# Four of the seven middle-sized tables looked up by TensorE in place of two, with the known rows in two buffers

## The reference, cut to what matters

```
e = stack([tbl_f[ids[:, f]] for f in range(50)], axis=1)      # 2048 x 50 x 16
z = einsum('bid,bjd->bij', e, e)[:, I, J]                     # pairs i < j: 1225
h = concatenate([z, dense_ctx], axis=1)                       # 1241
h = maximum(h @ W_top1 + b_top1, 0)                           # 512
h = maximum(h @ W_top2 + b_top2, 0)                           # 256
y = h @ W_top3                                                # 1
```

## Time and profile before

| | |
|---|---|
| three runs | 480.82, 483.11, 483.5 us |
| the profiled execution | 480.74 us, its span 478.8 us |
| mean granted TensorE clock | 0.857 of 2.4 GHz |
| PE / weight load busy | 332.1 / 233.1 us |
| DVE busy | 279.6 us |
| ACT busy | 196.2 us |
| POOL busy | 329.2 us |
| chain that ended last, by engine | PE 22%, SP queue 22%, DVE 14%, ACT 14%, DMA 9%, POOL 8%, issue 8% |

### The profile page before, as it was taken

The page is one execution under the profiler, slowest core; times in us unless marked ns, Lnnn a source line. Parts: engine busy times, 40 slices in busy tenths (PEclk is TensorE's granted clock), DMA queues, the critical chain, the costliest instruction groups (busy, mean ns, idle before and its releaser), DMA issues.

```text
span 478.8 us, 12641 instructions
## 1 busy us (share of the span) xinstructions
PE 332.1 (69%) x5432; PEld 233.1 (49%) x5432; DVE 279.6 (58%) x538; ACT 196.2 (41%) x269; POOL 329.2 (69%) x320
## 2 busy tenths in 40 slices
PE   0576154672978698889886697887969475574772
PEld 0576154662665466657654566565634142333331
DVE  3688599993543888484736967655342725435220
ACT  1427412543246544354483347344671322404020
POOL 5777878777777777777777777777777777750000
PEclk9768575886979979799997799999889797977798
DMA  6995332332222334222223322111212112120100
GB/s 190 404 344 156 109 95 60 75 100 62 65 69 51 101 92 105 79 81 56 54 73 103 86 52 48 40 35 38 60 15 62 37 40 52 21 62 3 58 1 0
DMA packets 24872, 38.70 MB, mean 81 GB/s; under 512 B 8784, under 2 KB 16240, under 8 KB 24688
## 3 DMA queue, kind: packets, MB, share of 16 engines
q1 hardware_dynamic: 14340, 34.80, 21.9%
q0 software_dynamic: 9984, 2.58, 6.1%
q10 hardware_dynamic: 492, 0.51, 0.3%
HBM read 26.79 MB, written 0.13 MB: 56 GB/s over the span
## 4 chain that ended last, share of the span: by engine, by line
PE 22%; SPq 22%; DVE 14%; ACT 14%; DMA 9%; POOL 8%; issue 8%; POOLq 0%; another core or an unknown queue 0%; ACTq 0%; DVEq 0%
SPq L358 22%; PE hid_ps L711 9%; POOL emb L426 8%; DVE onehot L460 6%; ACT gram L790 6%; PE look_ps L685 5%; DMA ids_bc<-ids_dram 5%; PE mid_ps L739 4%; ACT z_both L839 3%; PE gram_ps L702 3%; DMA z_both<-dense 2%; DVE turned L565 2%; ACT looked L809 2%; DVE z_both L522 1%; DVE w_sb L637 1%
## 5 line engine op out<-in xcount | busy, mean ns | idle before, releaser
L426 POOL DMA_INDIRECT emb<-tbl,gidx x312 | 328.4, 1053 | 97.4 <-issue 93.0
L711 PE MATMUL hid_ps<-w_sb,z_both 127*128 127x512 f16 x528 | 131.0, 398 | 17.0 <-DVE z_both L522 17.0
L685 PE MATMUL look_ps<-parts,onehot 125*128 125x64 f16 x1836 | 79.3, 207 | 67.0 <-DVE onehot L460 51.8
L685 PEld LDWEIGHTS look_ps<-parts,onehot 125*128 125x128 f16 x1836 | 73.2, 108 | 80.1 <-issue 37.0
L790 ACT ACTIVATE gram<-gram_ps 50x784 f32<-50x784 f32 x112 | 91.4, 816 | 45.1 <-PE gram_ps L702 41.7
L460 DVE TENSOR_SCALAR onehot<-ids_bc,rows 125x2048 f16<-125x2048 f16 (+1 forms) x144 | 92.4, 692 | 18.5 <-PE look_ps L685 14.7
L711 PEld LDWEIGHTS hid_ps<-w_sb,z_both 127*128 127x128 f16 x528 | 49.6, 102 | 76.3 <-DVE z_both L522 17.9
L702 PE MATMUL gram_ps<-turned 32*128 32x100 f16 x2048 | 37.4, 213 | 39.7 <-ACT gram L790 28.1
L809 ACT ACTIVATE looked<-look_ps 128x1024 f16<-128x1024 f32 (+1 forms) x28 | 26.7, 955 | 87.4 <-PE look_ps L685 87.3
L702 PEld LDWEIGHTS gram_ps<-turned 32*128 32x128 f16 x2048 | 27.0, 97 | 49.4 <-ACT gram L790 31.4
L460 DVE TENSOR_SCALAR onehot<-ids_bc,rows_med 125x1024 f16<-125x1024 f16 x75 | 34.6, 496 | 27.6 <-PE look_ps L685 27.5
(11 more groups left out here) (43 smaller groups left out, 128.9 us busy)
## 6 DMA issues: line engine op xcount, KB each, us to landing
ids_bc<-ids_dram SPq DMA_DIRECT2D x28, 512.0 KB, 4.1
emb<-tbl,gidx POOLq DMA_INDIRECT x312
z_both<-gram SPq DMA_DIRECT2D x31, 121.0 KB
z_both<-w SPq DMA_DIRECT2D x1, 2816.0 KB
z_both<-gram SPq DMA_DIRECT2D x31, 90.8 KB
z_both<-gram SPq DMA_DIRECT2D x155, 6.2 KB
z_both<-gram SPq DMA_DIRECT2D x31, 60.5 KB
gram<-small SPq DMA_DIRECT2D x2, 512.0 KB, 4.9
```

The costliest lines, as they stand in the source:

```text
L426: pool.indirect_dma_start(emb[:, T % TPC, f, :], None, big[f], bass.IndirectOffsetOnAxis(ap=gidx[:, T, f:f + 1], axis=0)).then_inc(gathere ...
L685: last = nc.tensor.matmul(bank[:, half, at:at + width], onehot[0:TP, at_ring, i, t * TILE:(t + 1) * TILE], moving.rearrange("p i s d -> p ...
L711: return nc.tensor.matmul(hid_ps[:, :], z_parts[0:KP, T % 2, x, k, :], w1_sb[0:KP, k, w, :], start=(i == 0), stop=(i == L1_MM - 1))
```

## The change

`NM` goes from 2 to 4: tables 26 and 27, the third and fourth in `MED`, are looked up by PE from chunk 1 on. Tiles 4 to 15 gather 17 fields in place of 19. A chunk from 1 on has 86 slices in place of 61 and 10 groups in place of 9, a slot 21 or 22 slices. `RING` goes to 5, `EARLY` to 14 and `MIDDLE` to 18.

The memory for this comes from other buffers. `looked` and `looked_med` become one ring of three groups (`LOOKS`), and a move of a group to its home follows two groups after its copy, in the chunk before the one that uses it. `split` becomes `known`, two halves by chunk parity, for rows that are looked up (and one gathered field that shares their last pair), and `fresh`, one tile's gathered rows for each of four tiles. The third copy is gone: the second transpose reads the two parts in reverse order. `odd` has two halves, loaded one chunk further ahead. The staging of the medium tables takes four places, two of them inside `parts_med`.

```diff
-NM = 2
+NM = 4
-RING = 6
+RING = 5
+LOOKS = 3
+JL = JS + JM + 1
-EARLY = 11
-MIDDLE = 13
+EARLY = 14
+MIDDLE = 18
-MOVES = ((0, 1), (2, 3), (4, 5), (6, 7), (8,), (), (), ())
-        odd = sb("odd", [128, TPC, PICK_BITS], I32)
+        odd = sb("odd", [128, 2, TPC, PICK_BITS], I32)
-        looked = sb("looked", [128, NG, 2, TPC, 2, PR, WORDS], F16)
-        looked_med = sb("looked_med", [128, NGM, MGRP, TPC, PRM, WORDS], F16)
+        looked = sb("looked", [128, LOOKS, 2 * TPC * 2 * PR * WORDS], F16)
-        split = sb("split", [128, TPC, JJ, 3, DIM, 2], F16)
+        known = sb("known", [128, 2, TPC, JL, 2, DIM, 2], F16)
+        fresh = sb("fresh", [128, TPC, JJ - JL, 2, DIM, 2], F16)
-        med_f32 = (parts_med[:, 1, :].bitcast(F32), gram[:, 0, 0:KM * DIM])
+        med_f32 = (parts_med[:, 1, :].bitcast(F32), gram[:, 0, 0:KM * DIM],
+                   parts_med[:, 3, :].bitcast(F32), gram[:, 1, 0:KM * DIM])
+        MED_HOME = (0, 2, 1, 3)
...
             def load_sample_ids(n):
-                if n > 0:
-                    sp.wait_ge(picked, FIRST_GROUP[n])
+                if n >= 2:
+                    sp.wait_ge(picked, FIRST_GROUP[n - 1])
...
+            load_sample_ids(1)
             for o in range(IDS_BUFS, FIRST_GROUP[1]):
                 load_ids_bc(o)
...
-            sp.dma_start(med_f32[0], med[:, 0, :]).then_inc(med_in[0], 16)
+            for m in (0, 2):
+                sp.dma_start(med_f32[m], med[:, MED_HOME[m], :]).then_inc(med_in[m], 16)
...
-            sp.dma_start(med_f32[1], med[:, 1, :]).then_inc(med_in[1], 16)
+            for m in (1, 3):
+                sp.dma_start(med_f32[m], med[:, MED_HOME[m], :]).then_inc(med_in[m], 16)
             for T in range(NTILES):
-                if T % TPC == 0 and T // TPC + 1 < NCH:
-                    load_sample_ids(T // TPC + 1)
+                if T % TPC == 1 and T // TPC + 2 < NCH:
+                    load_sample_ids(T // TPC + 2)
...
+            def homes(T):
+                t, half = T % TPC, T // TPC % 2
+                runs = [(emb[:, t, NM, :], known[:, half, t, JL - 1, :, :, 1])]
+                runs += [(emb[:, t, NM + 1 + a:NB:2, :], fresh[:, t, :, :, :, a]) for a in range(2)]
+                if T < TPC:
+                    runs += [(emb[:, t, a:NM:2, :], known[:, half, t, JS:JS + JM, :, :, a]) for a in range(2)]
+                return runs
...
             def split_rows(T):
...
-                known = JS + (JM if T >= TPC else 0)
-                if t == 0:
-                    dve.wait_ge(moved, FIRST_GROUP[T // TPC + 1])
-                    nc.vector.tensor_copy(
-                        split[:, :, 0:known, 2, :, :].rearrange("p t j d a -> p t j (d a)"),
-                        split[:, :, 0:known, 0, :, :].rearrange("p t j d a -> p t j (d a)"))
-                nc.vector.tensor_copy(
-                    split[:, t, known:JJ, 2, :, :].rearrange("p j d a -> p j (d a)"),
-                    split[:, t, known:JJ, 0, :, :].rearrange("p j d a -> p j (d a)")).then_inc(dve_step, 1)
...
             def turn(T):
+                dve.wait_ge(emb_read, T + 1)
+                if T % TPC == 0:
+                    dve.wait_ge(moved, FIRST_GROUP[T // TPC + 1])
...
-                src = split[:, T % TPC, :, :, :, :].rearrange("p j s d a -> p j (s d a)").bitcast(U32)
-                for buf, w0 in ((turned, 0), (turned2, DIM)):
-                    out = buf[:, T % 2, :, 0:NF].bitcast(U32).rearrange("p b j -> p j b")
-                    nc.vector.transpose(out, src[:, :, w0:w0 + WORDS]).then_inc(turned_ready, 1)
+                for src, j0, j1 in ((known[:, T // TPC % 2, T % TPC], 0, JL), (fresh[:, T % TPC], JL, JJ)):
+                    words = src.rearrange("p j s d a -> p j s (d a)").bitcast(U32)
+                    for buf, way in ((turned, 1), (turned2, -1)):
+                        out = buf[:, T % 2, :, 2 * j0:2 * j1].bitcast(U32).rearrange("p b j -> p j b")
+                        nc.vector.transpose(out, words[:, :, ::way, :]).then_inc(turned_ready, 1)
...
             def copy_lookups(n, q, banks=(look_ps,)):
                 o = FIRST_GROUP[n] + q
-                if n > 0:
-                    act.wait_ge(moved, FIRST_GROUP[n - 1] + min(q, len(groups_of(n - 1)) - 1) + 1)
+                if o >= LOOKS:
+                    act.wait_ge(moved, o - LOOKS + 1)
...
             def med_high(i):
                 act.wait_ge(med_in[i], 16)
-                if i > 0:
-                    act.wait_ge(med_lo, i)
+                if i >= 2:
+                    act.wait_ge(med_lo, 1 if i == 2 else i)
...
             def slot(T):
-                    if T >= TPC and T % TPC == 0:
-                        for q in MOVES[g]:
-                            move(T // TPC, q)
+                    if g == 0 and T >= TPC and T % TPC == 0:
+                        for q in groups_of(n - 1)[-2:]:
+                            move(n - 1, q)
...
                             if k == SLICES[q] - 1:
                                 copy_lookups(n, q)
+                                if q >= 2:
+                                    move(n, q - 2)
```

More of the change, by code:

```diff
@@ L251, in build @@
         ids_in = sem("ids_in")
-        sample_in = sem("sample_in")
+        sample_in = [sem(f"sample_in{i}") for i in range(2)]
         small_in = [sem(f"small_in{i}") for i in range(PLOADS)]
@@ L474, in pick @@
                         na = min(2, cnt - 2 * h)
-                        both = looked[:, q, h, :, 0:na, :, :].bitcast(U32)
+                        both = looked_small(o)[:, h, :, 0:na, :, :].bitcast(U32)
                         first = TABLES[q][0] + 2 * h
-                        mask = odd[:, :, first:first + na].unsqueeze(3)\
+                        mask = odd[:, n % 2, :, first:first + na].unsqueeze(3)\
                             .broadcast_to([128, TPC, na, WORDS // 2])
@@ L481, in pick @@
                 else:
-                    four = looked_med[:, q - NG, :, :, :, :].bitcast(U32)
+                    four = looked_med(o).bitcast(U32)
                     first = NS + TABLES[q][0]
                     def bit(at, width):
-                        return odd[:, :, at:at + MGRP].rearrange("p t a -> p a t").unsqueeze(3)\
+                        return odd[:, n % 2, :, at:at + MGRP].rearrange("p t a -> p a t").unsqueeze(3)\
                             .broadcast_to([128, MGRP, TPC, width])
@@ L497, in find_odd @@
             def find_odd(n):
[L499 to L501 removed]
+                dve.wait_ge(sample_in[n % 2], 16 * (n // 2 + 1))
+                nc.vector.tensor_scalar(odd[:, n % 2, :, 0:NS + NM], odd[:, n % 2, :, 0:NS + NM], 1, None, ALU.bitwise_and)
+                nc.vector.tensor_scalar(odd[:, n % 2, :, NS + NM:], odd[:, n % 2, :, NS + NM:], 2, None, ALU.bitwise_and)\
                     .then_inc(odd_made, 1)
@@ L535, in split_rows, with part @@
+            def part(home, x):
+                return home[:, x, :] if len(home.shape) == 3 else home[:, :, x, :]
             def split_rows(T):
[L537 to L540, removed]
+                dve.wait_ge(gathered[T % TPC], rows_gathered(T))
+                if T // TPC >= 2 and T % TPC == 0:
+                    dve.wait_ge(turned_ready, 4 * TPC * (T // TPC - 1))
+                for e, home in homes(T):
+                    last = nc.vector.tensor_scalar(part(home, 0), e, SCALE, None, ALU.mult)
@@ L541, in split_rows @@
                 last.then_inc(dve_step, 1)
-                dve.wait_ge(dve_step, 2 * T + 1)
-                for e, hi, lo in rows_by_parity(T):
-                    last = nc.vector.scalar_tensor_tensor(lo, e, SCALE, hi, ALU.mult, ALU.subtract)
+                dve.wait_ge(dve_step, T + 1)
+                for e, home in homes(T):
+                    last = nc.vector.scalar_tensor_tensor(part(home, 1), e, SCALE, part(home, 0), ALU.mult, ALU.subtract)
                 last.then_inc(emb_read, 1)
-                known = JS + (JM if T >= TPC else 0)
@@ L692, in dots @@
                 if e == 0:
[L693 removed]
+                    pe.wait_ge(turned_ready, 4 * T + 4)
                 if EVACS * T + e > 0:
@@ L813, in move @@
                 act.wait_ge(picked, FIRST_GROUP[n] + q + 1)
-                if q == 0 and n > 0:
-                    act.wait_ge(turned_ready, 2 * TPC * n)
+                if q == 0 and n > 1:
+                    act.wait_ge(turned_ready, 4 * TPC * (n - 1))
+                o, to = FIRST_GROUP[n] + q, known[:, n % 2]
                 if q >= NG:
                     last = nc.scalar.activation(
-                        split[:, :, JS + q - NG, 0:2, :, :].rearrange("p t s d a -> p t (s d) a"),
-                        looked_med[:, q - NG, :, :, 0, :].rearrange("p a t w -> p t w a"), ACT.Copy)
+                        to[:, :, JS + q - NG, :, :, :].rearrange("p t s d a -> p t (s d) a"),
+                        looked_med(o)[:, :, :, 0, :].rearrange("p a t w -> p t w a"), ACT.Copy)
                 else:
@@ L827, in move @@
```

(4 more changed lines are left out.)

26 lines of the change are left out of this document (11 added, 15 removed).

## The result

The changed kernel takes 505.24 us (502.62 to 508.68, four runs) against 482.28: 4.8% slower, ratio 1.048 with a 95% interval of 1.041 to 1.055. The forecast was 495 in a range of 479 to 509, so the direction and the range held, and the loss came out larger. The profiled execution took 502.62 us, its span 500.8, which is 22.0 us over the span of before; the sum of the prediction had 13.6.

The account below looks back on a forecast made before the run. The prediction took PE plus a stall at each chunk's start as the limit, gathers level with it. Its terms added 13.6 us to the profiled 480.7, giving 494.3, stated as 495 towards the median, range 479 to 509.

Parts of the forecast that it names:

- the sum: Length changes of the start, each slot and the tail added up: +13.6 us on the profiled execution's 480.7, giving 494.3.
- opening of slot 3: First matmul of dots(2) on PE, at 120.6 us before: start +5.5, slot 0's compares +4.1, ring and small +1.3.
- The limit: Between slots 3 and 12: PE plus a stall at each chunk's start bounds, gathers level with it, not ahead.
- the paragraph on the chunk's start: Slots 4 and 8: DVE's wait for `odd` goes, ScalarE's added copies cost nothing; both slots last 28 us.
- the ring of five: One-hot ring cut from 6 to 5: 0 where PE is the limit, 1 us in slot 0; bounds 0 to 1.
- The packing: Slots 9 to 11: 6.6 us stood for ScalarE's copies, behind it a packing not yet landed, which a longer slot covers.
- the two slow rivals: The stall stays, 504 us at chance 0.15, and DVE becomes the limit, 508 us at 0.17.
- Gathers are the limit: Lookups fit into PE's idle time and tiles 4 to 11 follow POOL's new pace: 457 us; chance 0.07.
- The clock: Denser work keeps PE's full clock everywhere, shortening slots 3, 4, 5, 8 and the tail: 484 us; chance 0.13.
- The stall stays: DVE meets another wait in place of `odd`; slots 4 and 8 gain nothing, 8 to 9 us: 504; chance 0.15.
- DVE becomes the limit: Reversed transposes cost double, 1.6 us a tile, 13 us over slots 0, 1, 4, 8 and eight others: 508; chance 0.17.
- The preparation: Start: casting and splitting two more tables before chunk 1 delays its compares 5.5 us; bounds 2 and 7.

Follow-up runs that it names:

- the aligned kernel: Changed kernel with the same 86 slices a chunk dealt so that each group ends where a position ends: 489.45 us, ratio 1.014 to the kernel before.

## Why the prediction was right, and where its size was off

By its own steps, forecast and measured on the profiled executions, in us of length added; the first row of the table is contained in the second:

| step | forecast | measured |
|---|---|---|
| start of chunk 1's compares | +5.5 | +4.9 |
| opening of slot 3 | +10.9 | +16.0 |
| slot 3 | +2.3 | -1.7 |
| slots 4 and 8 | -9.0 | -5.3 |
| slots 5 and 9 | +0.9 | +7.1 |
| slots 6 and 10 | +7.9 | +8.6 |
| slots 7 and 11 | +3.2 | +1.1 |
| slot 12, tail | -2.6 | -3.8 |
| span | +13.6 | +22.0 |

The limit. "Between slot 3 and slot 12 the limit is PE plus a stall at each chunk's start, and the gathers run level with it": right, and now shown from both sides. Taking 24 gathers away is worth 1.1%, the structure that takes the stall away nothing, both 3.9%.

Two steps failed. The first is in the paragraph on the chunk's start: "ScalarE gets three more copies ... so I cost these at nothing; the cover is that PE's first layer runs beside them". The cover was real before (slots 6 and 7 90% full of PE work), but I did not ask whether it stays. The change alters how many slices a position holds, and so where a group ends. In slots 4, 5, 8 and 9 PE's wait for ACT's copies went from 6.7 to 17.6 us, 10.9 more; forecast and measurement part there by 9.9 us; and where the deal of slices alone takes this wait away, these slots get 11.0 us shorter, some 10 without the slices that left them. The Trainium skill has a rule that points at this place ("Perfetto Trace Analysis", Matmuls): independent groups should rotate through different PSUM banks, so that one group's evacuation overlaps the next one's matmuls. The 1.18 us rows agree; other banks were not tried.

The second is in the sum: "Slots 1 and 2 swallow their extra slices: slot 1's 21 are partly narrow and medium". Slot 3's opening is 5.1 us later than forecast. From the first compare to the opening of slot 1 the added time is 5.0 us, near the 5.4 of the sum; slot 1 is 4.9 us longer (26.2 for 21.3) and slot 2 1.2, where the sum has nothing. Slot 1 had no room, since DVE was busy 98% of it before. Now it holds 1.6 us more of DVE's work and 3.0 us in which DVE stands for a place in the one-hot ring, while PE works at a granted clock of 0.61 and stands 7.2 us for one-hots and 2.4 for copies. In the aligned kernel slot 1 is 24.2 us with DVE busy 23.5: the copies account for some 2 us of the 4.9, DVE's own work for most of the rest. How much of it is the ring of five is open.

The packing was read as a wait that longer slots cover. That held for ACT's wait (14.4 us before, 10.1 after), but it is also a floor. Half the packing gives 11 us (8.4 between the profiled executions, in slots 2 and 12), and these slots are only 1.2 and 0.3 us longer than before; so it is hardly a part of the miss, and it hid what else could be won. In the changed kernel slots 3, 7 and 11 sit at 22.3 to 23.0 us with PE 95 to 97% busy, and they went the other way: slot 3 came out 4.0 us shorter than forecast, slots 7 and 11 together 2.1. No run explains this.

Luck. The forecast gave 489 to 500 its chance of 0.48, and 505.24 lies outside. It lies in the stated range only because that range took in the two slow rivals, and neither of their mechanisms is what happened.

The rivals. "Gathers are the limit" is refuted by 476.11 where it needed 458 to 465 for the same gathers. "The clock" held in its mechanism, the granted clock rose to 0.94 to 1.00 in slots 3 to 10, and not in its price: it saved PE some 15 us of busy time (25 us more in all for 40 of added lookups) and the waits took them. "The stall stays" named two of the right slots and, at 504, nearly the time; but slots 4 and 8 did gain 5.3 us, and what PE stands for there is ACT's copy (4.0 us in each) more than one-hots (2.1). "DVE becomes the limit" by reversed transposes is refuted by 52.8 us for 49.5.

The costs. 66 ns for a pair of weight load and 128-column matmul held (1.06 us over 16 in both kernels at the full clock). The preparation put chunk 1's first compare 4.9 us later, in its bounds of 2 to 7 and near the 5.5 taken.

## What to carry to other kernels

Before adding work to an engine that runs a hand-written order, list the places where it hands a buffer over, and see what lies behind each in the new order: here a copy of 1.0 us was cheap while eight of nine hand-overs in a chunk fell before other matmuls, and dealing the slices so that all ten do again was worth 16 us after a third slice had moved seven of them inside a position. Ask of every engine, not only of the limiting one, whether it has room where work is added: slot 1 was full of DVE's work. When two limits lie at one height, test them together: the gathers and the stall were worth 1% and 0% alone, and 4% as a pair, which also says how much a change that removes both may spend. And a work term that costs nothing when it is taken out, as PE's 20 us of matmuls did, need not be free: ask which chain it was level with, and what the granted clock did.

## What the runs showed that was not expected

PE's waits of 1.18 us at each hand-over lie 0.16 us over ACT's copy of 1.02, so what lies between them besides the copy is small. With PE standing for 6 of 30 us in many short waits, the granted clock stayed at 1.00 in slots 4 and 8; it was lower behind one long wait, as ahead of dots in slot 9 of the aligned kernel:

```profile
296.90 0.85 PE L720 MATMUL gram_ps<-turned 32*128 32x100 f16 x32 [3.37 <-ACT gram L808]
297.89 3.76 PE L757 MATMUL mid_ps<-w_sb,h_turned 128*128 128x256 f32 x8
```

The second layer takes 3.76 us behind that wait and 1.97 in slot 8 of the same kernel.
